# Graph attention with its edges split by partition, a segment maximum and sums as scans in place of the window merges

## The reference

```python
h = relu(layernorm(x))                      # x: 12500 x 128
h = (h @ W_node.T).reshape(N, 4, 32)
e = (edge_attr @ W_edge.T).reshape(E, 4, 32)   # E = 412500 edges, 64 features each
att = sum(concat([h[src], h[tgt], e], -1) * a, -1)      # one logit per edge and head
att = where(att > 0, att, 0.2 * att)
m = maximum(segment_max(att, tgt), 0.0)
ex = exp(att - m[tgt])
denom = segment_sum(ex, tgt) + (E - deg)[:, None] * exp(-m)
w = ex / denom[tgt]
out = x + segment_sum(w[:, :, None] * h[src], tgt)
```

## Time and profile before

| | us |
|---|---|
| time, median of 3 runs | 4975.6 |
| time, lowest and highest | 4969.8 and 4982.6 |
| the profiled execution, its span on the core | 6376.5 |
| the profiled execution, its own time | not listed beside its span |

### The profile page before, as it was taken

One profiled execution on the slowest core, in us unless ns is written; L12 is line 12 of the kernel. 1 busy time (PEld: TensorE's weight loads), 2 busy tenths in 40 slices (PEclk: granted clock), 3 DMA queues, 4 the chain that ended last, 5 costly groups with the idle time before them and its releaser, 6 DMA issues.

```text
span 6376.5 us, 88250 instructions
## 1 busy us (share of the span) xinstructions
PE 3777.9 (59%) x24835; PEld 3479.1 (55%) x24835; DVE 2605.6 (41%) x9904; ACT 1215.2 (19%) x3468; POOL 3285.7 (52%) x3330
## 2 busy tenths in 40 slices
PE   3466566666666666666666666666664555544554
PEld 3356555656655555655556655556654445544454
DVE  4333343333333334343343334334344545544454
ACT  2212121212212122121222212121221111111111
POOL 3644545444454444545445454544445567766763
PEclk7566676676666667666666666667666656666665
DMA  6422222222222222222222222222222222322222
GB/s 126 92 82 79 81 81 79 78 79 82 77 84 78 81 77 81 84 80 79 76 81 83 79 81 80 79 76 81 79 76 63 69 74 74 84 76 68 77 81 57
DMA packets 299939, 506.25 MB, mean 79 GB/s; under 512 B 127979, under 2 KB 169403, under 8 KB 299662
## 3 DMA queue, kind: packets, MB, share of 16 engines
q1 hardware_dynamic: 196750, 287.92, 14.9%
q0 software_dynamic: 103168, 218.10, 13.9%
HBM read 490.01 MB, written 15.75 MB: 79 GB/s over the span
## 4 chain that ended last, share of the span: by engine, by line
another core or an unknown queue 37%; PE 17%; issue 15%; DVE 14%; DVEq 9%; ACT 4%; SPq 1%; POOL 1%; DMA 1%; ACTq 1%; POOLq 0%
PE ps_acc L1043 6%; DVEq L285 5%; PE ps_ef L962 5%; DVE val L882 3%; PE ps_hot L1007 3%; DVE hot_t L767 2%; ACT hot L572 1%; POOL gath L489 1%; DVE acc L789 1%; PE ps_ef L963 1%; ACT hot L573 1%; PE ps_ef L956 1%; SPq L323 1%; DVE u L801 1%
## 5 line engine op out<-in xcount | busy, mean ns | idle before, releaser
L489 POOL DMA_INDIRECT gath<-rows_scratch,idx x3224 | 3222.6, 1000 | 2928.1 <-DVE val L882 1983.5
L1043 PE MATMUL ps_acc<-val,hot 128*128 128x137 f32 x8970 | 1816.6, 383 | 215.3 <-DVE val L882 108.5
L1043 PEld LDWEIGHTS ps_acc<-val,hot 128*128 128x128 f32 x8970 | 1726.5, 284 | 243.3 <-issue 122.1
L1007 PE MATMUL ps_hot<-identb,hot_t 128*128 128x128 bf16 x4485 | 729.7, 260 | 896.6 <-issue 847.9
L1008 PE MATMUL ps_tgt<-tcur,hot_t 128*128 128x12 bf16 x4485 | 645.4, 187 | 825.5 <-issue 823.3
L1007 PEld LDWEIGHTS ps_hot<-identb,hot_t 128*128 128x128 bf16 x4485 | 590.4, 147 | 976.5 <-issue 947.1
L1008 PEld LDWEIGHTS ps_tgt<-tcur,hot_t 128*128 128x128 bf16 x4485 | 592.0, 155 | 900.2 <-issue 899.0
L816 DVE TENSOR_TENSOR_SCAN runs_f<-pens,ps_runs 4x128 f32<-4x128 f32 x345 | 141.1, 409 | 2261.3 <-remote 2213.7
L882 DVE TENSOR_TENSOR val<-gath,weight 128x1664 f32<-128x1664 f32 x345 | 645.1, 1870 | 0.0
L962 PE MATMUL ps_ef<-w_att,efb 128*128 128x8 f32 x2976 | 589.9, 333 | 34.0 <-ACT efb L550 26.3
L962 PEld LDWEIGHTS ps_ef<-w_att,efb 128*128 128x128 f32 x2976 | 566.7, 290 | 49.7 <-ACT efb L550 31.2
(11 more groups left out here) (172 smaller groups left out, 3451.5 us busy)
## 6 DMA issues: line engine op xcount, KB each, us to landing
hot_t<-dst_i_scratch SPq DMA_DIRECT2D x345, 416.0 KB
efb<-in_edge_attr_dram SPq DMA_DIRECT2D x247, 416.0 KB
gath<-rows_scratch,idx POOLq DMA_INDIRECT x3224
rows_scratch<-gath SPq DMA_DIRECT2D x14, 462.0 KB, 6.3
pens<-carry_scratch SPq DMA_DIRECT2D x345, 4.0 KB
att_e<-in_x_dram SPq DMA_DIRECT2D x6, 896.0 KB
out_dram<-att_e SPq DMA_DIRECT2D x6, 896.0 KB
att_e<-dst_f_scratch SPq DMA_DIRECT2D x1, 1860.0 KB
```

What stands on the lines that cost most here:

```text
L489: pool.indirect_dma_start(gath[:, k * J + j, :], None, rows[:, :], bass.IndirectOffsetOnAxis(ap=idx[:, half, k, j:j + 1], axis=0)).then_in ...
L1007: tp(hotp[j // 8][:, j % 8 * P:(j % 8 + 1) * P], t, identb[:, :])
L1043: last = mm(ps_acc[:, 0:VC], hot[:, q, j, :], val[:, j, :], start=(j == 0), stop=(j == J - 1))
```

## The change

The whole kernel is written anew around another division of the edges.

- Partition p owns 3224 neighbouring edges of the list (T), taken in 248 blocks of 13. There are no windows and no items. A block's running maximum and running sums of a target go on in the same partition from block to block.
- The maximum of a run so far is a scan over 4 x 14 (`mcols`). The sums are one scan over 132 x 14 = 1848 elements with a factor and a term each (`sums`). The factor, made by ScalarE into the PSUM tensor `A`, is exp(old maximum - new maximum), or 0 where a new target begins. The term is weight x gathered row (the product, 1716 elements); its weights `w_exp` lie in PSUM too.
- After each block ScalarE copies the states of all its edges (`copy_state`), and SP stores them to the DRAM table `state_scratch`. At the end GpSimd picks up the state at the last edge of each node with 98 gathers, 128 nodes each. Where a run crosses from one partition to the next a scan across the 128 partitions and one row per partition set it right.
- The target's part of the logit no longer comes by one-hot tiles. Each node's part is scattered once to the place of its first edge (98 scatters), the table is loaded back, and a scan spreads it over the run (`targets`). The places come from counting: 99 sign sums on ScalarE, 99 gathers of 806 targets each per partition, 99 compare-and-count operations on VectorE.
- GpSimd's 3224 gathers of rows (now 136 numbers) are written out one after another, without a loop. Their indices are loaded once (`idx`, 128 x 3224).
- The host lays out its inputs differently before the launch: x and the edge features come transposed as well, the edge list padded, the constants as inputs. TensorE transposes neither features nor nodes.

The core of the diff: constants, GpSimd, ScalarE and VectorE in the loop, and TensorE's and SP's part.

```diff
+T = 3224
+KB = 13
+BLOCKS = T // KB
+SLOTS = 4
+VAL = H * HB
+ROW = VAL + H
+COL = KB + 1
...
-                    for j in range(J):
-                        pool.indirect_dma_start(gath[:, k * J + j, :], None, rows[:, :],
-                                                bass.IndirectOffsetOnAxis(ap=idx[:, half, k, j:j + 1], axis=0)).then_inc(gather_dma[k], 16)
...
+            for k in range(W + 1):
+                if k % 9 == 0:
+                    pool.wait_ge(chunk_ready, k // 9 + 1)
+                if k >= RING:
+                    pool.wait_ge(chunk_used, k - RING + 1)
+                gather(ring[:, k % RING, :], dst16[:, :], chunk_i[:, k:k + 1], chunk_dma[k % RING])
+            rstd_of(0)
+            rstd_of(1)
...
+            for g in range(STEPS):
+                pool.wait_ge(rows_ready, g + 1)
+                for n in range(NG):
+                    k = g * NG + n
+                    scatter(tdst_d[:, :], put_i[:, k:k + 1], tnode[:, k, :], scattered)
...
+            for i in range(BLOCKS):
+                s = i % SLOTS
+                after(pool, val_done, i - SLOTS + 1)
+                for j in range(KB):
+                    gather(slots[:, s * KB + j, :], rows[:, :], idx[:, i * KB + j:i * KB + j + 1], gather_dma[s])
...
+            pool.wait_ge(val_done, BLOCKS)
+            gather(s_first[:, :], state_d[:, :], fe_i[:, 0:1], fix_gather)
+            for g in range(STEPS):
+                if g >= 7:
+                    pool.wait_ge(group_done, g - 6)
+                for n in range(NG):
+                    k = g * NG + n
+                    gather(slots[:, k % 49, :], state_d[:, :], get_i[:, k:k + 1], get_dma[g])
...
+            def body(it, q):
+                i = it * UN + q
+                v = q % 2
+                act.wait_ge(d_ready, i + 1)
+                after(act, val_done, i - 1)
+                nc.scalar.activation(w_exp[v], D1[:, v, :], ACT.Exp).then_inc(w_ready, 1)
+                after(act, scanned, i)
+                nc.scalar.activation(a_all.rearrange("p (h v t) -> p h v t", h=H, v=HB),
+                                     D2[:, v, :].rearrange("p (h a t) -> p h a t", h=H, a=1).broadcast_to([P, H, HB, COL]),
+                                     ACT.Exp).then_inc(a_ready, 1)
+                if not (isinstance(i, int) and i == 0):
+                    copy_state(i - 1, 1 - v, it, q)
...
+                nc.scalar.copy(R[:, k, :, :], vcols(k)[:, :, 1:COL].rearrange("p c t -> p t c")).then_inc(copied, 1)
...
+            def logits(it, q):
...
+                dve.wait_ge(gather_dma[s], it * (32 * KB) + 16 * KB * (q // SLOTS + 1))
+                nc.vector.tensor_tensor(hk(z[:, :]), slots[:, s * KB:(s + 1) * KB, VAL:ROW].rearrange("p t h -> p h t"),
+                                        td[:, ds(i * KB, KB), :].rearrange("p t h -> p h t"), ALU.add)
...
+                after(dve, copied, i - 1)
+                nc.vector.tensor_tensor_scan(mcols(v), pen[:, ds(i, 1), :, :].rearrange("p a h t -> p (a h t)"), att[:, :], 0.0, ALU.min, ALU.max)
...
+                nc.vector.tensor_copy(hk(att[:, :])[:, :, 0:1], hk(mcols(v))[:, :, KB:COL])
...
+            def sums(b, k, s, fresh):
+                dve.wait_ge(w_ready, b + 1)
+                v4 = vcols(k)[:, 0:VAL, :].rearrange("p (h v) t -> p h v t", h=H)
+                nc.vector.tensor_tensor(v4[:, :, :, 1:COL],
+                                        slots[:, s * KB:(s + 1) * KB, 0:VAL].rearrange("p t (h v) -> p h v t", h=H),
+                                        w_exp[k].rearrange("p (h a t) -> p h a t", h=H, a=1).broadcast_to([P, H, HB, KB]),
+                                        ALU.mult).then_inc(val_done, 1)
...
+                    nc.vector.tensor_copy(vcols(k)[:, 0:VAL, 0:1], vcols(1 - k)[:, 0:VAL, KB:COL])
+                dve.drain()
+                dve.wait_ge(a_ready, b + 1)
+                nc.vector.tensor_tensor_scan(V[:, k, 0:VAL * COL], a_all, V[:, k, 0:VAL * COL], 0.0, ALU.mult, ALU.add).then_inc(scanned, 1)
...
+            def body(it, q):
+                first_block = isinstance(it, int) and q == 0
+                logits(it, q)
+                if isinstance(it, int) and q < PIECES - 1:
+                    targets(q + 1)
+                if not first_block:
+                    sums(it * UN + q - 1, 1 - q % 2, (q - 1) % SLOTS, isinstance(it, int) and q == 1)
...
+                    for n in range(KB):
+                        last = mm(ps_ae[k][:, n * 2 * H:(n + 1) * 2 * H], eab[:, k, n * P:(n + 1) * P], w_att[:, :], start=True, stop=True)
...
+            def store(b, k):
+                sp.wait_ge(copied, b + 1)
+                sp.dma_start(state_rows[:, ds(b * (KB * ROW), KB * ROW)], R[:, k, :, :].rearrange("p t r -> p (t r)")).then_inc(store_dma[k], 16)
```

More of the change, by code:

```diff
@@ L3, with graph_attention_kernel @@
 from contextlib import ExitStack
-def graph_attention_kernel(nc, x, src, dst, edge_attr, w_node, w_edge, att_vec, out):
+P = 128
+N = 12500
+E = 412500
+D = 128
+H = 4
+HD = 32
+K = 64
+W = 98
+NP = P * W
+T = 3224
+KB = 13
+BLOCKS = T // KB
+PAIRS2 = BLOCKS // 2
+SLOTS = 4
+HB = HD + 1
+VAL = H * HB
+ROW = VAL + H
+COL = KB + 1
+CL = 512
+CE = P * T // CL
+SENTINEL = 16000
+BIG = 2.0 ** 126
+EPS = 1e-5
+NG = 7
+STEPS = W // NG
+UN = 8
+ITERS = BLOCKS // UN
+RING = 8
+PIECES = 8
+PT = T // PIECES
+def graph_attention_kernel(nc, x, x_t, src, dstf, dst16, lasts, ends, first, ea, w_node, w_node_t, a_blk, we2,
+                           ident_c, centre_c, cols_c, out):
     fp32, bf16, i32, i16 = mybir.dt.float32, mybir.dt.bfloat16, mybir.dt.int32, mybir.dt.int16
@@ L155, in graph_attention_kernel @@
[L155 to L163, removed]
@@ new lines, in _ @@
+            loop(sp, body)
+            store(EB - 1, 1)
+            sp.wait_ge(d_ready, EB)
+            for m in range(STEPS // 2):
+                a, b = m * 2 * NG, (m + 1) * 2 * NG
+                sp.dma_start(xr[:, a:b, :], x.rearrange("(p w) d -> p w d", p=P)[:, a:b, :]).then_inc(x_again[m], 16)
+            o = out[0:NP, :].rearrange("(p w) d -> p w d", p=P)
+            for g in range(STEPS):
+                sp.wait_ge(group_done, g + 1)
+                sp.dma_start(o[:, g * NG:(g + 1) * NG, :], xr[:, g * NG:(g + 1) * NG, :]).then_inc(stored, 16)
@@ new lines, in _ @@
+            centring(0)
+            pe.wait_ge(w_copied, 1)
+            for g in range(STEPS):
+                if g + 1 < STEPS:
+                    centring(g + 1)
+                pe.wait_ge(squared, g + 1)
+                for n in range(NG):
+                    last = mm(var_p[g // 7][:, g % 7 * NG + n:g % 7 * NG + n + 1], sq[g % 2][:, n * P:(n + 1) * P], ones[:, :], start=True, stop=True)
+                last.then_inc(var_done, 1)
+            pe.wait_ge(var_copied, 2)
+            for g in range(STEPS):
+                after(pe, rows_ready, g)
+                for a, b, bank in proj:
@@ L1024, in _ @@
-            run_ends(0, 0)
-            tiles(0, 0)
-            carry(0)
-            def body(k, q, make):
-                i = 2 * k + q
-                if not is_last(i):
-                    run_ends(i + 1, 1 - q)
-                    if make:
-                        transpose_ef(i + 4, q, ef_count(k, q))
-                    tiles(i + 1, 1 - q)
-                    carry(i + 1)
-                if make:
-                    edge_logits(i + 4, q)
-                pe.wait_ge(val_done, i + 1)
-                pe.wait_ge(hot_done, i + 1)
-                after(pe, sums_copied, i)
-                for j in range(J):
-                    last = mm(ps_acc[:, 0:VC], hot[:, q, j, :], val[:, j, :], start=(j == 0), stop=(j == J - 1))
-                last.then_inc(summed, 1)
```

1345 lines of the change are left out of this document (545 added, 800 removed).

## The result

Ran beside the kernel before, the changed kernel takes **4534.06 us** (median of 4 runs, 4533.43 to 4534.55) against 4978.66 (4 runs, 4969.78 to 4982.64): ratio 0.9113, 95% interval 0.91 to 0.9126. The forecast was 4515.

The account below looks back on a forecast made before the run. The prediction took GpSimd's issue of gathers, lengthened by VectorE's hold, as the bound. Start 285, gathers 4030, hold 40 and tail 160 summed to 4515 us; range 4360 to 4800.

Parts of the forecast that it names:

- The bound: GpSimd's issue of 3224 gathers sets the pace, 1.25 us from start to start, 4030 us in the loop.
- The hold: VectorE operations with two SBUF inputs lengthen gathers starting within them; 735 us before, 40 after, bounds 0 to 124.
- the 735 us: Kernel before: median 4975.6 less start, gathers and end, laid to VectorE's hold on gathers, 2.13 us per item.
- The ends: Before the first loop gather 285 us (was 150.7), after the last gather 160 us (was 60).
- The chain under the cover: VectorE and ScalarE in the loop take 11.2 us a block, at worst 14.9, hidden under 16.25 us of gathers.
- A: GpSimd's 1.25 us step is partly the profiler's; at 1.0 us a step the time is 3635 us; chance 0.06.
- C: GpSimd's step itself is 1.48 us when timed, VectorE's hold no part of it: 5280 us; chance 0.07.
- B: VectorE and ScalarE's chain per block exceeds 16.25 us; at 17.5 a block 4785 us; chance 0.10.
- D: Start and tail swell to 340 and 200 us through full queues: 4610 us; chance 0.77 together with the forecast.
- the reading of the 6376.5 us: Kernel before's profiled execution: its extra 1.4 ms sits in stalls of other engines, so terms use the 4975.6 us median.

Follow-up runs that it names:

- e1: Kernel after with the product's weights moved from PSUM back to SBUF, the long scan's factors still in PSUM: 5102.47 us.
- e3: Kernel before with its weights moved from SBUF to PSUM, the carries moved to another bank: 6757.45 us, 1.0672 of the kernel before there.
- a0: Kernel after, unchanged, run again on another chip: 5156.15 us, 0.8021 of the kernel before there.
- f3: Kernel after with TensorE's loop halved to 4 blocks and VectorE's product done twice a block: 5296.25 us.
- e5: Kernel after with VectorE's product done four times a block, the same result written again: 6426.4 us.

## Why the prediction was right, and where it was not

**The bound.** Right for the kernel after: GpSimd. Its step, 1.25 forecast, was 0.957 + 0.305 = 1.262. For the kernel before in the prompt condition it remains argued: there is no trace of it there.

**The hold.** Right in mechanism: put back into the kernel after it costs 2.14 us per product (e1), and taken out of the kernel before it is gone (e3). Its size there, the 735 us, stays a remainder; the estimate above gives 618 to 704 for the products, and what makes the rest, L767's hold or something else, wasn't told apart. In the kernel after hardly anything of the hold is left: the 3224 gathers are busy 3086.4 us, 8 more than at their median of 0.955, where 40 were set down. The step came out 0.012 us above 1.25, 39 us over 3224, and so the sum of the two terms, 4070, met 4067.7. That is luck: an error in one was covered by an error in the other. The Trainium skill (SBUF — State Buffer, Who interferes with whom) infers that a `tensor_tensor` doesn't hold descriptor generation; e1 disagrees with it, 3.13 us against 0.95. The same section says that one with two SBUF inputs does contend with GpSimd's reads of SBUF. A gather reads its indices there, and no run here separates the two.

**The ends.** Start 285, measured 293.2; tail 160, measured 171.3. The powers took 8.2 us each, not 10.4.

**The chain under the cover.** Too short on paper: 11.2 us a block, measured 13.8. Mis-sized were the product (3.24 for 1.93) and ScalarE's copy (3.19 for 1.6); both read with a stride, which may be why, but no run changed it. The scan took 4.01, and the sum of 8.4 had used 3.9 for it. Two sums don't come out of their terms: the small operations with the short scan make 1.95 at their lowest prices and not 1.75, and a slower read with a doubled copy makes 11.2 + 1 + 1.6 = 13.8 and not 14.9. That 13.8 is also what was measured is chance in part, since the product came out 1.3 longer and not 1. It lay 2.6 us below the gathers' 16.4, where 5 had been counted on, so nothing came of it. One reads this margin from VectorE's wait: 6.37 us a block for gathers (1579.9 / 248), of which some 4.2 would else be waited for ScalarE's copy, as L548 does in a0.

**The rivals.** A (a shorter step) and C (1.48): the step is 1.262. B: 13.8 is below 16.4; one more product, 17.1, and f3 is bound by it outside its late stretches. D: 293 and 171, nowhere near 340 and 200.

**The step that failed** is the reading of the 6376.5 us: "whose extra 1.4 ms sits in stalls of other engines", taken for the profiler's doing and left out of the forecast. The stalls are there, but not the profiler's: on three chips the kernel before takes such a time run after run. So the profiled execution was most likely of the late condition (its span and TensorE's pauses fit) and the three timed ones of the prompt one. The forecast was for the prompt one and holds there, and that the result was timed there too is luck. In the late one the kernel after takes 5156, outside the range, and the gain is larger (0.80). There the bound of the kernel after is TensorE's lateness with VectorE's chain, not GpSimd, so the gain must have another cause than the one forecast. Likely it is that the old kernel sends 24835 matmuls through a TensorE that starts some of them late, and the new one 3685; no run shows it.

**Open:** what makes TensorE late on some chips, why the stretch comes once in eight blocks whatever its own program looks like, and why e1 and e5 have it only at the start. That this lateness is the whole difference between 4534 and 5156 fits the waits (1457.9 us for L541, less what VectorE would have waited for gathers) and is argued, not shown.

## What to carry to other kernels

Where GpSimd issues gathers back to back, look at VectorE's long operations with both inputs in SBUF; here one small operand in PSUM instead of SBUF took 2.1 us of hold out of each, and the product itself was no faster. Count the instructions of the engine that bounds, since half the rows saved only 5% of a gather. And where a profiled execution is far from the timed ones, get its own time before blaming the profiler: here it was, as far as the runs tell, another chip's condition, in which another engine is the bound.

## What the runs showed of the hardware that I had not expected

- The same program takes 4978 or 6360 to 6445 us by the chip, and this one 4534 or 5156; within a chip the runs of the one agree to 2% (6389.97 to 6517.79) and of the other to 0.2%. What the traces of the kernel after show to differ is TensorE, whose instructions start 1.4 or 2.1 us apart for a while, and a first gather some 20 us later (315.9 for 293.2).
- A VectorE product with both inputs in SBUF holds a gather: 3.13 us for 0.95 (e1); with one input in PSUM it doesn't (mean 956 ns beside 13 us of products a block in e5).
- An indirect gather costs 910 ns for 64 rows and 957 for 128, with a gap of 0.30.
- VectorE's scan with multiply and add takes 4007 ns for 1848 elements; its strided product 3241 for 1716; a power on GpSimd 8202 ns for 49 columns and 1480 for 7.
